# The first layer's scan inputs: softplus with a sign-bit pass and one combined pass on DVE, and no GpSimd addition

## The reference, cut to what matters

```
u = silu(causal_conv1d(xm, conv_w, conv_b))          # 4 taps for each channel
dt, Bm, Cm = split(u @ xproj_w.T, [6, 22])
delta = softplus(dt @ dtproj_w.T + dtproj_b)
# the scan then reads u, delta, delta*u, Bm, Cm
```

## Time and profile before

| | us |
|---|---|
| median of three runs | 22473.82 |
| lowest, highest | 22467.68, 22474.48 |
| the profiled execution's own time | 22468.44 |
| its span in the profile | 22466.7 |
| forward stage of scan inputs | about 537 to 1100 |
| backward stage of scan inputs | about 3704 to 4263 |

### The profile page before, as it was taken

How to read it: one execution, slowest core, us unless ns; L and a number is a source line. 1 busy time by engine, 2 the same in 40 slices (tenths; PEclk the granted TensorE clock), 3 DMA queues, 4 the chain that set the end, 5 groups by cost and what they waited for, 6 DMA issues and landing times. The chain is left out here.

```text
span 22466.7 us, 264583 instructions
## 1 busy us (share of the span) xinstructions
PE 19369.5 (86%) x73736; PEld 10093.5 (45%) x73736; DVE 17043.7 (76%) x13056; ACT 16452.2 (73%) x25994; POOL 13494.5 (60%) x5860
## 2 busy tenths in 40 slices
PE   7788887788886889989998988889899888889798
PEld 2344443344442334434445555555555555235353
DVE  2777777777775659937669999999999998446666
ACT  6488886688882455556569999999999998124545
POOL 0277774377771558806349999999999998000101
PEclk8699998799996899998679999999999999569899
DMA  4566665566666341174543333333333333520202
GB/s 123 187 206 191 204 193 177 191 204 194 203 198 175 91 162 77 62 260 186 198 178 121 121 121 121 121 120 115 118 122 121 120 122 111 134 76 28 84 29 79
DMA packets 842186, 3171.46 MB, mean 141 GB/s; under 512 B 101515, under 2 KB 124541, under 8 KB 815750
## 3 DMA queue, kind: packets, MB, share of 16 engines
q1 hardware_dynamic: 805510, 3029.73, 41.2%
q10 hardware_dynamic: 35328, 125.85, 1.7%
HBM read 2316.32 MB, written 838.88 MB: 140 GB/s over the span
## 5 line engine op out<-in xcount | busy, mean ns | idle before, releaser
L1525 DVE TENSOR_TENSOR_SCAN l1s_h<-l1s_da,l1s_pd 128x1024 f32<-128x1024 f32 x3072 | 6862.7, 2275 | 389.5 <-PE l1s_pd L1460 378.6
L1556 ACT ACTIVATE l1s_dm<-l1s_dut,l1s_bt 128x384 f32<-128x384 f32 x8192 | 4449.7, 605 | 16.6 <-DMA l1s_u<-u 11.3
L1460 PE MATMUL l1s_pd<-l1s_id,l1s_dm 128*128 128x128 f32 x24576 | 3197.1, 277 | 609.9 <-ACT l1s_dm L1556 358.3
L1460 PEld LDWEIGHTS l1s_pd<-l1s_id,l1s_dm 128*128 128x128 f32 x24576 | 2756.3, 142 | 2033.7 <-DVE l1s_h L1525 1061.2
L1546 ACT ACTIVATE l1s_da<-l1s_dl,l1s_a 128x1024 f32<-128x1024 f32 x3072 | 3504.0, 1141 | 18.4 <-DVE l1s_h L1525 17.1
L1436 POOL TENSOR_TENSOR l1s_sm<-l1s_h 128x1024 f32<-128x1024 f32 x1024 | 2429.0, 2372 | 264.6 <-DVE l1s_h L1525 253.9
L1441 POOL TENSOR_TENSOR l1s_pb<-l1s_h,l1s_cc 128x1024 f32<-128x1024 f32 x1024 | 2433.4, 2376 | 1.1
L1445 POOL TENSOR_TENSOR l1s_pa<-l1s_sm,l1s_cc 128x1024 f32<-128x1024 f32 x1024 | 2428.8, 2372 | 0.0
L2318 POOL TENSOR_TENSOR l0sb_pr<-l0sb_h,l0sb_cc 128x1024 f32<-128x1024 f32 x768 | 1812.2, 2360 | 775.7 <-DVE l0sb_h L2391 718.0
L2318 POOL TENSOR_TENSOR l0sf_pr<-l0sf_h,l0sf_cc 128x1024 f32<-128x1024 f32 x768 | 1812.1, 2360 | 774.9 <-DVE l0sf_h L2391 713.6
L849 POOL TENSOR_TENSOR dw_acc<-dw_acc,dw_prod 128x961 f32<-128x961 f32 (+3 forms) x704 | 1572.8, 2275 | 1092.6 <-ACT dw_prod L802 1085.0
(11 more groups left out here) (291 smaller groups left out, 31044.3 us busy)
## 6 DMA issues: line engine op xcount, KB each, us to landing
l1s_cc<-crows SPq DMA_DIRECT2D x1024, 512.0 KB, 3.7
l0sf_cc<-l0crowsf SPq DMA_DIRECT2D x512, 512.0 KB, 5.0
l0sb_cc<-l0crowsb SPq DMA_DIRECT2D x512, 512.0 KB, 5.0
l0sf_cc<-l0crowsf SPq DMA_DIRECT2D x512, 256.0 KB, 6.4
l0sb_cc<-l0crowsb SPq DMA_DIRECT2D x512, 256.0 KB, 6.3
dls<-l1p_dl SPq DMA_DIRECT2D x192, 512.0 KB, 6.9
duts<-l1p_dut SPq DMA_DIRECT2D x64, 1536.0 KB, 7.0
l1s_dut<-duts SPq DMA_DIRECT2D x64, 1536.0 KB, 7.2
```

Of the source, the lines that this page charges most:

```text
L1460: mm = pe.transpose(pd[:, s % 2, blk * 128:blk * 128 + 128], dm[:, rnd % 2, blk, j * 128:j * 128 + 128], idt[:, :])
L1525: dve.tensor_tensor_scan(h[:, s % 4, :], da[:, j, :], pd[:, s % 2, :], 0.0, ALU.mult, ALU.add)\
L1556: ins = act.activation(dm[:, rnd % 2, blk, :], dut[:, half, blk, :], ACT.Identity, scale=bt[:, half, blk, n:n + 1])
```

## The change

- L403's pass is gone. In its place `minus_abs(t)` is one DVE pass: it reads `pd` as 32-bit integers and sets the sign bit with a bitwise or, which gives -|x| in `ab`. It waits for `dtm` (PE's x) and for ACT's Exp of the item before.
- A new `softplus(t)` is one DVE pass: max(`pd`, 0) + `ln` into `dl`. It waits for `lnd` (ACT's Ln of the same tile), and for t = 0 for the store that frees `dl`.
- The POOL block is gone. `sumd` is now raised by DVE.
- The order on DVE changes from `times_u, convolve, minus_abs` to `times_u, minus_abs, convolve, softplus`.
- PE's `deltas` waits for `sumd` instead of `absd` before it writes a `pd` buffer again, since `softplus` is now the last reader.

```diff
-            @block.gpsimd
-            def _(pool):
-                def turn(k, s):
-                    for t in range(T):
-                        pool.wait_ge(lnd, nth(T * k + t))
-                        pool.tensor_tensor(dl[:, s % 2, t, :], dl[:, s % 2, t, :], ln[:, t, :], ALU.add).then_inc(sumd, 1)
-
-                turns(pool, turn, 0, 0, UNROLL, ITEMS)
-
...
                     def minus_abs(t):
 
-                        if not here(k):
-                            return
-                        if t == 0:
-                            dve.wait_ge(s_dl[p], (k - p) * 8)
-                        dve.wait_ge(dtm, nth(T * k + t))
-                        dve.tensor_scalar(dl[:, p, t, :], pd[:, (s + t) % 2, :], 0.0, None, ALU.max).then_inc(plus, 1)
-                        dve.wait_ge(plus, nth(T * k + t))
-                        dve.wait_ge(expd, nth(T * (k - 1) + t))
-                        dve.scalar_tensor_tensor(out=ab[:, t, :], in0=dl[:, p, t, :], scalar=-2.0, in1=pd[:, (s + t) % 2, :],
-                                                 op0=ALU.mult, op1=ALU.add).then_inc(absd, 1)
+                        if here(k):
+                            dve.wait_ge(dtm, nth(T * k + t))
+                            dve.wait_ge(expd, nth(T * (k - 1) + t))
+                            dve.tensor_scalar(ab[:, t, :].bitcast(I32), pd[:, (s + t) % 2, :].bitcast(I32), SIGN, None, ALU.bitwise_or).then_inc(absd, 1)
+
+                    def softplus(t):
+
+                        if here(k):
+                            if t == 0:
+                                dve.wait_ge(s_dl[p], (k - p) * 8)
+                            dve.wait_ge(lnd, nth(T * k + t))
+                            dve.scalar_tensor_tensor(out=dl[:, p, t, :], in0=pd[:, (s + t) % 2, :], scalar=0.0, in1=ln[:, t, :],
+                                                     op0=ALU.max, op1=ALU.add).then_inc(sumd, 1)
 
                     for t in range(T):
                         times_u(t)
+                        minus_abs(t)
                         convolve(t)
-                        minus_abs(t)
+                        softplus(t)
                     convolve(3)
...
                         pe.wait_ge(dtc, nth(2 * k + 1))
-                        pe.wait_ge(absd, nth(T * k + t - 2))
+                        pe.wait_ge(sumd, nth(T * k + t - 2))
```

More of the change, by code:

```diff
@@ L21 @@
 F8 = mybir.dt.float8e5
+I32 = mybir.dt.int32
 ALU = mybir.AluOpType
@@ L267, in here @@
         return there(k, ITEMS)
+    SIGN = -2 ** 31
     with ExitStack() as stack:
@@ L288, in l0_scan_inputs @@
         s_du = [r.dma_sem(f"du{p}") for p in range(2)]
-        const, taps, conv, silu, xd, dtc, btm, btc, dtm, plus, absd, expd, lnd, sumd, dud, dutm, dutc, passed = r.step_sems(
-            "const", "taps", "conv", "silu", "xd", "dtc", "btm", "btc", "dtm", "plus", "absd", "expd", "lnd", "sumd",
+        const, taps, conv, silu, xd, dtc, btm, btc, dtm, absd, expd, lnd, sumd, dud, dutm, dutc, passed = r.step_sems(
+            "const", "taps", "conv", "silu", "xd", "dtc", "btm", "btc", "dtm", "absd", "expd", "lnd", "sumd",
             "dud", "dutm", "dutc", "passed")
```

## The result

The changed kernel takes 22605.4 us (median of four, 22601.9 to 22617.2) against 22470.8 us before (four, 22459.0 to 22474.5). The ratio is 1.0062, its 95% interval 1.0044 to 1.0079: 0.6% slower, where 22617 was forecast. The profiled execution took 22617.2 us, the longest of the four.

A forecast was written before the change was run, and what follows sets the result against it. DVE was taken to set the pace, with one wait for PE. Turns 1 to 13 at 38.3 instead of 33.66 us plus 11 at the edges made 71.5 us a direction, 143 for both: 22473.8 + 143 = 22617 us, range 22495 to 22710.

The forecast's parts named there:

- The POOL pass: DVE's tap groups: without POOL's pass beside them, each of three groups gives back 2.14 us, 6.4 us a turn.
- The new order: DVE behind times_u: waits for the whole round trip through PE three times a turn, 6.98, 4.3 and 7.0 us.
- The parts of a turn: Turns 1 to 13: 11.60 us first tile, 10.20 each for the others, 3.62 last taps; 35.6 us at full clock.
- the upper bound for the sign pass: DVE's sign pass: taken as 1.14 us, at most 0.07 us more, or +7 us over 96 passes.
- The clock at the third tile: PE ahead of turn_du(2): a 3.6 us gap drops it to 1.2 GHz, adding 2.7 us, for 38.3 a turn.
- The edges: Turns 14 and 15, without taps: 2.2 us more for five of six tiles, 11 us a direction.
- Both trips at full clock: Rival, second and third tiles on PE at 2.4 GHz: 36.5 us more a direction, 22547 us; chance 0.2.
- The low clock for both: Rival, second and third tiles on PE at 1.2 GHz: 106.4 us more a direction, 22687 us; chance 0.17.
- the full clock for the first tile: Rival, PE's first tile also at full clock: a turn of 32.9 us, 22476 us, not slower; chance 0.1.
- long taps without POOL: Rival, DVE's taps stay long: 6.4 us more a turn, 44.7 us, 22782 us; chance 0.03.

The follow-up runs named there:

- e6: The kernel before with POOL's addition cut to one column of each tile, all waits and order kept: 22333.0 us, ratio 0.9941 to before.
- e1: The changed kernel with one swap on PE, deltas(t) ahead of turn_du(t): 22313.3 us, ratio 0.9930 to the kernel before.
- e2: The changed kernel with DVE's old order, convolve(t) ahead of minus_abs(t), and softplus a tile later; PE unchanged: 22329.3 us, ratio 0.9938 to the kernel before.
- e5: The kernel before with only DVE's order changed, minus_abs(t) ahead of convolve(t), POOL's addition kept: 22709.9 us, ratio 1.0107 to before.
- e3: The changed kernel with the matrix products of project(1) issued twice, filling PE's gap ahead of turn_du(2): 22569.2 us, ratio 1.0044 to the kernel before.
- e4: The kernel before with one swap on PE, deltas(t) ahead of turn_du(t): 22350.3 us, ratio 0.9948 to before.
- e8: The changed kernel with deltas(t) first on PE and ACT's copy turned(t) moved behind Exp and Ln: 22369.8 us, ratio 0.9957 to the kernel before.
- e7: The changed kernel with convolve(t) ahead of minus_abs(t) and softplus a tile later on DVE, deltas(t) ahead of turn_du(t) on PE: 22262.0 us, ratio 0.9908 to before.

## Why the prediction was right

- **The POOL pass.** Forecast: 2.14 us back for each group of three taps, 6.4 us a turn. Measured 88 us a stage. Of the 42 groups that had a POOL pass near them 41 held a lengthened tap (in the first turn it was POOL's own pass that grew, to 3.12 us): 2.14 us each. e6 shows the cause alone.
- **The new order.** Forecast: the trip through transposes and x exposed three times. Shown by the three waits and by e1, e2 and e5. Before, e5, e2 and the changed kernel give the order's price: with POOL's pass 22710 - 22471 = 239 us, without it 22605 - 22329 = 276. POOL's pass was worth 142 us in the old order and 105 in the new one, since there the first of its three passes fell into a wait.
- **The parts of a turn.** First tile 6.98 forecast, 790.99 - 784.01 = 6.98 measured. Second 4.3, measured 4.31. Third 7.0, measured 6.89 in the turn shown. Sign pass and sum 1.14 each from start to start, measured 1.14. One reading beside it was wrong and changed nothing: from the start of L403 to that of L406 it is 773.60 - 772.34 = 1.26 us, and not at most 1.22, so the upper bound for the sign pass should have been 0.05 us higher.
- **The clock at the third tile.** Forecast: 0.50. Right in 7 of 13 turns of the forward stage (a wait of 5.68 us); in the other six the wait was 4.10 to 4.51, so the clock fell partway through the trip. That is the term that was most off: 38.3 us a turn forecast, 37.57 measured, 0.73 x 13 x 2 = 19 us too much. The edges came to 63.6 - 13 x 3.91 = 12.8 us a direction instead of 11. So the two stages gave 127 us where 143 were forecast. That the medians differ by 134.6, nearer to it, is in part luck: the rest came from outside both stages, where the prediction had said that nothing moves.
- **The rivals.** Both trips at full clock is what e3 made by force: turn 35.7 (35.6 forecast), 22569 us (22547 forecast). The low clock for both, the full clock for the first tile and long taps without POOL didn't occur. One reason given against the full clock for the first tile was false: PE does not idle longer ahead of `turn_du(0)` than before, but 3.83 us in the turn shown, where it was 7.99. The clock was at 0.50 there all the same: it had fallen to it in the turn before and rose only in `project(0)`.
- **What the forecast didn't see**: that mending the order gives more than the POOL pass alone. It compared the change with the kernel before, in which the same trip cost 120 us (e4).

## What to carry to other kernels

When a pass is moved on one engine, write down the whole way from the instruction ahead of it, through the other engines' queues, back to what it waits for: work that stood between the two was cover. If the consumer's input doesn't depend on the producer, look in the other engine's queue for the place where the two were chained only by order, as `deltas` was behind `turn_du`; swapping them gave 120 us in the kernel before and 292 us in the changed one. A saving on a shared resource and a cost in order add only nearly, so time each alone and both together; and before moving a copy earlier or later, list everything that waits for it, also what only needs its source tile free (e8).

## What the runs showed of the hardware

PE's clock fell while PE was at work. In e7, stretches of PE alone:

```profile
core 0: us, PE busy (x), PEclk, DMA share, GB/s
...
764.10:767.10 3.00, 3.00 (x17) 1.00 0.30 37
768.40:771.00 2.60, 2.60 (x18) 0.70 0.73 295
771.00:773.20 2.20, 2.20 (x12) 0.50 0.86 363
774.30:778.90 4.60, 4.60 (x12) 0.50 0.64 249
```

PE was busy throughout `turn_b` (K = 16, 16 columns), 1.21 us of idle time stood ahead of it, and the clock went from 1.00 to 0.50 in it. It came back in `project(0)` (K = 128), in each of turns 1 to 13. e2 shows the fall with no idle time at all. PE works there from 761.43 to 789.65 us without a gap, and `turn_b` starts at 782.88:

```profile
core 0: us, PE busy (x), PEclk, DMA share, GB/s
772.93:783.17 10.24, 10.24 (x41) 1.00 0.47 82
783.20:789.60 6.40, 6.40 (x31) 0.50 0.61 250
```

The fall lies in `turn_b` in each of turns 1 to 13 of e2. So work without a gap did not keep the clock up here. Why it falls in `turn_b` no run shows. The Trainium skill, TensorE: Matmul & The Clock Gate, section HAM oscillation — how this bites in real kernels, tells of the fall through waits between bursts; the gap of 3.61 us in the changed kernel and e3 agree with that, and the fall inside `turn_b` in e2 and e7 goes beyond it.

A pass of POOL and a DVE pass that both read two SBUF tiles held each other up in either order: a tap that came second took 3.37 us instead of 1.21, a POOL pass that came second 3.25 instead of 2.34 (e5).
